# Chunk-wise loading with a k-major first projection, squares on ScalarE, and a later place for the LayerNorm statistics

## The chip, the cores and the metric

The kernel runs on the 8 cores of one Trainium2 chip. Each core takes 2,048 of the 16,384 tokens and does the whole layer for them; the cores exchange nothing. The time is device microseconds of the slowest core. The kernel before takes 786.37 us, the median of 3 runs (785.95 to 786.61).

## The reference

```python
def attn(query):                      # D = 1024, 16 heads of 64, M = 3 levels
    qkv = query @ W_qkv.T + b_qkv
    q, v = qkv[..., :D], qkv[..., 2*D:]            # per head: [B, H, L, 64]
    cq, cv = haar_wavedec(q, 3), haar_wavedec(v, 3)  # along L
    prod = [cq[j]*wq[j] * (cv[j]*wv[j]) for j in range(3)] + [cq[3]*cv[3]]
    a = prod[0]
    for d in prod[1:]:
        a = haar_idwt_step(a, d)
    return a @ W_out.T + b_out
def ffn(x):                           # hidden 3072, int weights * 1/127
    return (silu(x @ wg.T) * (x @ wu.T)) @ wd.T
x = layernorm(x + attn(x))            # LayerNorm 1
x = layernorm(x + ffn(x))             # LayerNorm 2
```

Everything is kept transposed: the 1024 features lie on partitions in 8 chunks of 128, the tokens along the free dimension, in 4 groups (g) of 512. A LayerNorm therefore needs sums over partitions, and these are made on TensorE: a matmul with a matrix that holds 1/1024 everywhere gives the mean (line 548), a second one over the squares the mean square (line 554).

## The kernel before, in words

The kernel is written as a list of operations for each of the five engines. The order of the calls in the Python text is the order of the instructions on each engine, and a small planner (`_Plan.op`) turns the reads and writes of each operation into semaphore waits. An operation may name whole groups of buffers as one resource: `r_ysq` stands for all eight tiles of squares, and `r_ybfp[g % 2]` for the eight bf16 tiles of one token group. DMAs go out on two queues, SyncE's (`DQ`) and GpSimd's (`GQ`); a queue's issues are in the order of the text.

Stage 1, loading and projection. The 8 MB of x come in four DMAs of two chunks each, chunks 0 to 3 on SyncE's queue and 4 to 7 on GpSimd's, and behind them on GpSimd's queue the first weight slabs. Each chunk is cast to bf16, the even ones by ScalarE (line 321), the odd ones by VectorE (line 327). For every output chunk c, `proj_chunk` makes q and then v: for each of the 4 token groups 8 matmuls (k = 0 to 7, line 367) into one of PSUM banks 0 to 3, and one ScalarE eviction (line 374). Then `mixer(c)` runs 18 VectorE operations, the Haar transform, products and the inverse; the first two read all of q and v, and the evictions of the next q wait for them.

Stage 2, output projection and LayerNorm 1. `wout_group(g)` makes 8 output chunks (oc) of 8 matmuls each (line 475). The first group runs k = 0 to 6 of all eight while the last mixer works, and k = 7 afterwards. Behind each chunk stands a tail: ScalarE evicts the bank (line 487), VectorE adds x (line 493), VectorE squares the sum (line 495). Most VectorE operations carry the line of the helper `tt`, line 266. In groups 1 to 3 the tails of the first three chunks are held back, and ahead of them the callback `_mid_stats` puts the statistics of the group before: 16 matmuls into banks 4 and 5, an eviction of the mean (line 563), two VectorE operations for the variance, Ln and Exp on ScalarE (lines 568, 571), one more on VectorE. The statistics of group 3 follow in the FFN, at hc = 1. The normalization of a group, 2 casts and 16 operations on VectorE (lines 588 to 596), is put behind all tails of the next group (`flush_norm`).

Stage 3, the FFN, twice over two token groups: gate and up matmuls (line 722), Silu on ScalarE (line 731), the product on VectorE (line 736); then the down projection, 24 matmuls for each output chunk (line 755). Its tail is an eviction (line 765), steps of LayerNorm 2 of the group before, an add on VectorE (line 771), a cast on ScalarE (line 775) and a square on VectorE (line 779).

Of the kernel before, what the change touches and what calls it, by code (L numbers as in the profile page):

```python
# [10 lines left out]
AF = mybir.ActivationFunctionType  # L11
ALU = mybir.AluOpType
# [107 lines left out]
def _build_nc():  # L120
    nc = bass.Bass("TRN2", target_bir_lowering=False)

    x_d = nc.dram_tensor("x", [128, NCH * TOK], F32, kind="ExternalInput").ap()
    wq_d = nc.dram_tensor("wq", [NCH, 128, 8 * 128], F32, kind="ExternalInput").ap()
# [53 lines left out]
    o_xbf = S0  # L178
# [48 lines left out]
    P = _Plan()  # L227
# [36 lines left out]
    def tt(out, i0, i1, op, reads, writes):  # L264
        P.op("vector", "dve", 1,
             (lambda e, out=out, i0=i0, i1=i1, op=op: e.tensor_tensor(out=out, in0=i0, in1=i1, op=op),  # L266
              tuple(reads), tuple(writes)))
# [38 lines left out]
                                 in_=biasp_d.rearrange("(c p) k -> p c k", p=128)),  # L306
           (), (r_bias,))
    rXdq, rXgq = _Res(), _Res()
    for h in range(4):
        sl = slice(h * 2 * TOK, (h + 1) * 2 * TOK)  # L310
        Q = DQ if h < 2 else GQ
        wr = ((rXc[2 * h], rXc[2 * h + 1])
              + ((rXdq,) if h == 1 else (rXgq,) if h == 3 else ()))
        Q.dma(lambda e, sl=sl: e.dma_start(out=Xflat[:, sl], in_=x_d[:, sl]),
              (), wr)

    xbf = v16(o_xbf, NCH * TOK)
    for c in range(NCH):
        if c % 2 == 0:
            P.op("scalar", "act", 1,  # L320
                 (lambda e, c=c: e.activation(out=xbf[:, c * TOK:(c + 1) * TOK],  # L321
                                              in_=X3[:, c, :], func=AF.Identity,
                                              bias=0.0, scale=1.0),
                  (rXc[c],), (rxbf[c],), tuple(rXg)))
        else:
            P.op("vector", "dve", 1,
                 (lambda e, c=c: e.tensor_copy(xbf[:, c * TOK:(c + 1) * TOK],  # L327
                                               X3[:, c, :]),
                  (rXc[c],), (rxbf[c],), tuple(rXg)))
    P.op("vector", "dve", 1,  # L330
         (lambda e: e.tensor_copy(cons[:, 15:16], cons[:, 5:6]),
          (rXdq, rXgq, r_consts), tuple(rXg)))

    wf3 = v32(o_wfeat, 48).rearrange("p (c k) -> p c k", k=6)
    al3 = v32(o_alpha, 32).rearrange("p (c k) -> p c k", k=4)
# [47 lines left out]
    def mixer(c):  # L383
# [32 lines left out]
        tt(me, a1.rearrange("p (b i) -> p b i", i=4), d1q.rearrange("p (b i) -> p b i", i=4), ALU.add, [rc], [r_mixc[c]])  # L416
        tt(mo, a1.rearrange("p (b i) -> p b i", i=4), d1q.rearrange("p (b i) -> p b i", i=4), ALU.subtract, [rc], [r_mixc[c]])

    for c in range(NCH):
        wap, wres = stream_slab(wq_d[c])  # L420
        proj_chunk(c, wap, wres, qt, r_qt, 0, xbf, rxbf)
        wap, wres = stream_slab(wv_d[c])
        proj_chunk(c, wap, wres, vt, r_vt, 1, xbf, rxbf)
        woap, wores = stream_slab(wo_d[c])
        DQ.dma(lambda e, c=c, woap=woap: e.dma_start(out=wos_d[c], in_=woap),
               (wores,), (r_wos[c],))
        mixer(c)
# [54 lines left out]
    def _wout_tail(g, oc, bank, ybfp):  # L482
        es_ = etmp_rr[0] % 6
        etmp_rr[0] += 1
        tmp = v32(o_etmp + 2048 * es_, TG)
        P.op("scalar", "act", 1,
             (lambda e, bank=bank, tmp=tmp, oc=oc: e.activation(  # L487
                 out=tmp, in_=pb[bank], func=AF.Identity,
                 bias=bias3[:, oc, 2:3], scale=1.0),
              (r_pb[bank], r_bias), (r_etmp[es_],)))  # L490
        xsl = v32(o_X + (oc * TOK + g * TG) * 4, TG)
        ybf_w = [r_ybfp[g % 2]] + (r_wosl_e[2:] if g == 1 else [])
        tt(ybfp[:, oc * TG:(oc + 1) * TG], tmp, xsl, ALU.add,
           [r_etmp[es_], rXg[g]], ybf_w)
        tt(_sq_ap(oc), ybfp[:, oc * TG:(oc + 1) * TG], ybfp[:, oc * TG:(oc + 1) * TG],
           ALU.mult, [r_ybfp[g % 2]], [r_ysq])

    PBANKS = [0, 1, 2, 3, 6, 7, 4, 5]

    def wout_group(g, mid_cb=None):  # L500
        ybfp = v16(o_ybf + 8192 * (g % 2), NCH * TG)
        if g == 0:
            info = {}
            for oc in range(NCH):
                wbf, wres = wout_slab(g, oc)
                bank = PBANKS[oc]
                info[oc] = (bank, wbf, wres)
                _wout_mm(g, oc, bank, wbf, wres, list(range(7)), True, False)
            for oc in range(NCH):
                bank, wbf, wres = info[oc]  # L510
                _wout_mm(g, oc, bank, wbf, wres, [7], False, True)
                _wout_tail(g, oc, bank, ybfp)
            wout_rr[0] = 0
        else:
            held = []
            for oc in range(NCH):
                wbf, wres = wout_slab(g, oc)
                bank = WBANKS[wout_rr[0] % 6]
                wout_rr[0] += 1
                _wout_mm(g, oc, bank, wbf, wres, list(range(8)), True, True)  # L520
                if oc < 3:
                    held.append((oc, bank))
                    if oc == 2:
                        if mid_cb:
                            mid_cb()
                        for hoc, hbank in held:
                            _wout_tail(g, hoc, hbank, ybfp)
                        held = []
                else:
                    _wout_tail(g, oc, bank, ybfp)  # L530
# [166 lines left out]
    for hh in range(2):  # L697
# [41 lines left out]
        for gi in range(2):  # L739
            g = 2 * hh + gi  # L740
            pg = g % 2
            ybase = y2off[pg]
            for oc in range(NCH):
                par = wd_slot[0] % 4
                wd_slot[0] += 1
                GQ.dma(lambda e, oc=oc, par=par: e.dma_start(  # L746
                           out=v16(o_wdbf + 6144 * par, 3072), in_=wd_d[oc]),
                       (), (r_wdbf[par],))
                wdbf_ap = v16(o_wdbf + 6144 * par, 3072)
                bank = dwn_rr[0] % 4  # L750
# [28 lines left out]
                tt(_sq_ap(oc), y2bfp[:, oc * TG:(oc + 1) * TG],
                   y2bfp[:, oc * TG:(oc + 1) * TG], ALU.mult, [r_ybfp[pg]], [r_ysq])  # L780
            pending_stages.extend(ln2_stages(g))

    flush_ln2()
# [73 lines left out]
```

How the kernel before makes its waits and increments, by code:

```python
            def body(h_, eng=eng):  # L789
                for builder, waits, incspec in P.ops[eng]:
                    for s, v in waits:
                        h_.wait_ge(sems[s], v)
                    if builder is not None:
                        ins = builder(h_)
                        if incspec is not None:
                            ins.then_inc(sems[incspec[0]], incspec[1])
```

## Time and profile before

| what | value |
|---|---|
| median of 3 runs | 786.37 us |
| the profiled execution's own time | 787.92 us |
| its span, slowest core (core 6) | 786.3 us (all cores 781.2 to 786.3) |
| PE matmuls busy | 701.7 us, 89% of the span |
| VectorE (DVE) busy | 320.1 us, 41% |
| ScalarE (ACT) busy | 195.0 us, 25% |
| GpSimd (POOL) busy | 65.2 us, 8% |

The page has one column for each fortieth of the span (19.7 us). PE's busy tenths are `0199999978887999999999999999999999999980`, VectorE's `0218888875787521221221225433322211121546`: the first column without matmuls is the load of x, columns 9 to 13 hold stage 2, and the last column is the end of LayerNorm 2. Matmul busy time says that PE had matmuls in flight, not how fast they ran; the granted clock of a stretch stands in rows of its own. L266 is a helper's line, so VectorE rows are told apart by tiles: `t_sc<-t_fsc,t_X` is the add of stage 2, `t_sc<-t_sc 128x512 bf16` there the square.

### The profile page before, as it was taken

Reading aid. Unit: us, or ns where it says so; the run is one execution under the profiler, and the core shown is the slowest. Engines: PE = TensorE matmul, PEld = TensorE weight load, DVE = VectorE, ACT = ScalarE, POOL = GpSimd, SP = SyncE. Lnnn points to the kernel's source line nnn. Section 1 sums busy time; section 2 is a strip of 40 time slices with the busy share of each in tenths; the row PEclk is TensorE's granted clock in tenths of the full one; section 3 lists DMA queues with packets and bytes.
Section 4 is the critical chain, followed back from the end, with each engine's and each line's share of the span. In section 5 each row is a group of like instructions: output and inputs, shape, how many; then the busy total and the mean of one; then the engine's idle time right before and its main releaser. Section 6 shows DMA issues by size and latency. Waiting matters only on the chain.

```text
span 786.3 us, 9771 instructions; the slowest of 8 cores (781.2 to 786.3 us)
## 1 busy us (share of the span) xinstructions
PE 701.7 (89%) x3136; PEld 315.1 (40%) x3200; DVE 320.1 (41%) x524; ACT 195.0 (25%) x295; POOL 65.2 (8%) x113
## 2 busy tenths in 40 slices
PE   0199999978887999999999999999999999999980
PEld 0034444433332444444444444444444444444430
DVE  0218888875787521221221225433322211121546
ACT  0234343324332311111111232331111111123220
POOL 1001011000001011100110101001101111010000
PEclk9999999999997999999999999999999999999995
DMA  8915444353312222222252437223332225244512
GB/s 231 251 28 94 68 81 81 94 150 81 84 49 88 74 81 66 69 81 80 81 188 81 161 121 216 93 80 113 102 108 81 81 80 188 79 140 143 174 55 107
DMA packets 33936, 84.56 MB, mean 108 GB/s; under 512 B 4704, under 2 KB 4704, under 8 KB 33376
## 3 DMA queue, kind: packets, MB, share of 16 engines
q0 software_dynamic: 21408, 60.82, 26.7%
q1 hardware_dynamic: 12480, 23.11, 9.7%
q8 instruction: 28, 0.46, 0.2%
q14 instruction: 20, 0.16, 0.1%
HBM read 54.56 MB, written 10.49 MB: 83 GB/s over the span
## 4 chain that ended last, share of the span: by engine, by line
PE 80%; DVE 10%; DMA 5%; issue 2%; ACT 2%; another core or an unknown queue 0%; DVEq 0%; SPq 0%; ACTq 0%; POOLq 0%
PE pb L722 42%; PE pb L755 20%; PE pb L367 14%; DVE t_sc L266 5%; DMA t_X<-x 4%; PE pb L548 2%; PE pb L554 1%; DVE t_fsc L266 1%; DVE t_ntmp L266 1%; DVE t_ntmpbf L266 1%; PE pb L475 1%; DVE t_var L266 1%; ACT t_sc L321 0%; DMA t_sc<-wgu 0%
## 5 line engine op out<-in xcount | busy, mean ns | idle before, releaser
L722 PE MATMUL pb<-t_sc 128*128 128x512 bf16 x1506 | 332.7, 381 | 6.5 <-DMA t_sc<-wgu 4.9
L722 PEld LDWEIGHTS pb<-t_sc 128*128 128x128 bf16 x1536 | 150.7, 98 | 188.2 <-issue 8.5
L755 PE MATMUL pb<-t_h,t_mix 128*128 128x512 bf16 x752 | 165.2, 379 | 3.6 <-DVE t_h L736 2.8
L736 DVE TENSOR_TENSOR t_h<-pb,t_sg 128x512 bf16<-128x512 f32 x96 | 66.4, 691 | 232.3 <-PE pb L722 221.2
L367 PE MATMUL pb<-t_sc 128*128 128x512 bf16 x502 | 114.7, 388 | 38.6 <-DMA t_sc<-wq 36.4
L731 ACT ACTIVATE t_sg<-pb 128x512 f32<-128x512 f32 x96 | 57.1, 597 | 254.6 <-PE pb L722 237.7
L755 PEld LDWEIGHTS pb<-t_h,t_mix 128*128 128x128 bf16 x768 | 75.0, 98 | 93.7 <-issue 3.6
L266 DVE TENSOR_TENSOR t_sc<-t_sc 128x512 bf16<-128x512 bf16 (+3 forms) x144 | 83.0, 577 | 63.7 <-ACT t_sc L775 30.3
L367 PEld LDWEIGHTS pb<-t_sc 128*128 128x128 bf16 x512 | 50.8, 99 | 102.0 <-issue 44.0
L701 POOL DMA_DIRECT2D t_sc<-wgu x48 | 33.8, 705 | 390.8 <-PE pb L722 287.4
L475 PE MATMUL pb<-t_mix,t_sc 128*128 128x512 bf16 x250 | 58.8, 394 | 8.2 <-ACT t_fsc L487 5.9
L374 ACT ACTIVATE t_sc<-pb,t_bias 128x512 bf16<-128x512 f32 x64 | 44.0, 687 | 69.2 <-PE pb L367 48.9
L475 PEld LDWEIGHTS pb<-t_mix,t_sc 128*128 128x128 bf16 x256 | 25.6, 101 | 41.0 <-issue 13.4
L765 ACT ACTIVATE t_dtmp<-pb 128x512 f32<-128x512 f32 x32 | 19.0, 595 | 91.9 <-PE pb L755 86.0
L266 DVE TENSOR_TENSOR t_X<-t_dtmp,t_sc 128x512 f32<-128x512 f32 x16 | 11.1, 693 | 57.0 <-ACT t_dtmp L765 57.0
L746 POOL DMA_DIRECT2D t_mix<-wd x32 | 17.0, 536 | 158.3 <-PE pb L755 153.6
L548 PE MATMUL pb<-t_sc,t_ones 128*128 128x512 bf16 x63 | 17.1, 416 | 9.0 <-DVE t_sc L266 6.5
L487 ACT ACTIVATE t_fsc<-pb,t_bias 128x512 f32<-128x512 f32 x32 | 19.4, 693 | 18.8 <-PE pb L475 18.1
L266 DVE TENSOR_TENSOR t_sc<-t_fsc,t_X 128x512 bf16<-128x512 f32 x32 | 22.1, 692 | 4.6 <-ACT t_fsc L487 1.6
L327 DVE CAST t_sc<-t_X 128x2048 bf16<-128x2048 f32 x4 | 4.7, 1224 | 30.2 <-DMA t_X<-x 30.2
L554 PE MATMUL pb<-t_sc,t_ones 128*128 128x512 bf16 x63 | 16.4, 406 | 0.0
L266 DVE TENSOR_TENSOR t_fsc<-t_dtmp,t_sc 128x512 f32<-128x512 f32 x16 | 11.0, 690 | 12.9 <-ACT t_dtmp L765 12.4
(39 smaller groups left out, 211.8 us busy)
## 6 DMA issues: line engine op xcount, KB each, us to landing
t_sc<-wgu POOLq DMA_DIRECT2D x48, 512.0 KB, 3.7
t_mix<-wd POOLq DMA_DIRECT2D x32, 768.0 KB, 4.2
t_sc<-wos SPq DMA_DIRECT2D x32, 256.0 KB, 3.0
t_X<-x POOLq DMA_DIRECT2D x2, 2048.0 KB, 21.8
t_X<-x SPq DMA_DIRECT2D x2, 2048.0 KB, 26.3
y<-t_X SPq DMA_DIRECT2D x8, 512.0 KB, 3.7
y<-t_fsc SPq DMA_DIRECT2D x8, 512.0 KB, 2.8
t_sc<-wq POOLq DMA_DIRECT2D x8, 256.0 KB, 5.5
```

The costliest lines, as they stand in the source:

```text
L266: (lambda e, out=out, i0=i0, i1=i1, op=op: e.tensor_tensor(out=out, in0=i0, in1=i1, op=op), tuple(reads), tuple(writes)))
L367: lambda e, bank=bank, k=k, g=g, wbf=wbf: e.matmul(pb[bank], wbf[:, 128 * k:128 * (k + 1)], rhs_ap[:, k * TOK + g * TG: k * TOK + (g + 1) ...
L374: (lambda e, bank=bank, g=g, c=c, dst_ap=dst_ap, bcol=bcol: e.activation(out=dst_ap[:, g * TG:(g + 1) * TG], in_=pb[bank], func=AF.Identit ...
L475: lambda e, bank=bank, k=k, g=g, wbf=wbf, s=start, st=stop, ks=ks: e.matmul(pb[bank], wbf[:, 128 * k:128 * (k + 1)], mix[:, k * TOK + g * ...
L487: (lambda e, bank=bank, tmp=tmp, oc=oc: e.activation(out=tmp, in_=pb[bank], func=AF.Identity, bias=bias3[:, oc, 2:3], scale=1.0), (r_pb[ba ...
L548: parts.append((lambda e, c=c, bm=bm: e.matmul(pb[bm], ones_ap, bfap[:, c * TG:(c + 1) * TG], start=(c == 0), stop=(c == NCH - 1)), (r_one ...
L554: parts.append((lambda e, c=c, bs=bs: e.matmul(pb[bs], ones_ap, _sq_ap(c), start=(c == 0), stop=(c == NCH - 1)), (r_ones, r_ysq), (r_pb[bs ...
L701: GQ.dma(lambda e, hc=hc, par=par: e.dma_start(out=_wgu_slot_ap(par).rearrange("p (w f) -> p w f", f=1024), in_=wgu_d[hc].rearrange("w p f ...
L722: lambda e, bank=bank, wsel=wsel, k=k, g=g, wgubf_ap=wgubf_ap: e.matmul(pb[bank], wgubf_ap[:, wsel * 1024 + 128 * k: wsel * 1024 + 128 * ( ...
L731: (lambda e, gbank=gbank, sgap=sgap: e.activation(out=sgap, in_=pb[gbank], func=AF.Silu, bias=0.0, scale=S_DEQ), (r_pb[gbank],), (r_sg[pid ...
L736: (lambda e, hsl=hsl, sgap=sgap, ubank=ubank: e.tensor_tensor(out=hsl, in0=pb[ubank], in1=sgap, op=ALU.mult), (r_pb[ubank], r_sg[pidx]), ( ...
L755: lambda e, bank=bank, hc=hc, gi=gi, wdbf_ap=wdbf_ap: e.matmul(pb[bank], wdbf_ap[:, 128 * hc:128 * (hc + 1)], h[:, hc * 1024 + gi * TG: hc ...
```

## The change

Four edits. x comes in eight DMAs of one chunk, four on each queue, and the two weight slabs of output chunk 0 are issued ahead of them. Output chunk 0 has a projection of its own, `proj_chunk0`: k is the outer loop and all eight banks (4 for q, 4 for v) accumulate at once; the evictions come with the last k. The squares of stage 2 and of the down projection move from VectorE to ScalarE (activation `Square`), right behind the add or the cast. In groups 1 to 3 of stage 2 six tails are held back, not three, so the statistics stand behind the sixth chunk.

```diff
-    for h in range(4):
-        sl = slice(h * 2 * TOK, (h + 1) * 2 * TOK)
-        Q = DQ if h < 2 else GQ
...
-        Q.dma(lambda e, sl=sl: e.dma_start(out=Xflat[:, sl], in_=x_d[:, sl]),
-              (), wr)
+    def _load_x_and_cast():
+        for c in range(NCH):
+            Q = DQ if c < 4 else GQ
+            wr = (rXc[c],) + ((rXdq,) if c == 3 else (rXgq,) if c == 7 else ())
+            Q.dma(lambda e, c=c: e.dma_start(out=Xflat[:, c * TOK:(c + 1) * TOK],
+                                             in_=x_d[:, c * TOK:(c + 1) * TOK]),
+                  (), wr)
...  (the casts, as before)
+    def proj_chunk0(w0q, w0v):
+        streams = ((w0q[0], w0q[1], qt, r_qt, 0), (w0v[0], w0v[1], vt, r_vt, 1))
+        for k in range(7):
+            for si in range(2):
+                wap, wres = streams[si][0], streams[si][1]
+                for g in range(NG):
+                    bank = 4 * si + g
+                    P.op("tensor", "pe", 1,
+                         (lambda e, bank=bank, k=k, g=g, wap=wap: e.matmul(
+                             pb[bank], wap[:, 128 * k:128 * (k + 1)],
+                             xbf[:, k * TOK + g * TG: k * TOK + (g + 1) * TG],
+                             start=(k == 0), stop=False),
+                          (wres, rxbf[k]), (r_pb[bank],)))
+        for si in range(2):
...
+            for g in range(NG):
+                bank = 4 * si + g
...  (the matmul of k = 7 into this bank, then its eviction by ScalarE)
+        bank_rr[0] = 0
+
+    w0q = stream_slab(wq_d[0])
+    w0v = stream_slab(wv_d[0])
+    _load_x_and_cast()
     for c in range(NCH):
+        if c == 0:
+            proj_chunk0(w0q, w0v)
+        else:
...  (slab q, proj_chunk, slab v, proj_chunk, as before)
         woap, wores = stream_slab(wo_d[c])
...
@@ _wout_tail
-        tt(_sq_ap(oc), ybfp[:, oc * TG:(oc + 1) * TG], ybfp[:, oc * TG:(oc + 1) * TG],
-           ALU.mult, [r_ybfp[g % 2]], [r_ysq])
+        P.op("scalar", "act", 1,
+             (lambda e, oc=oc, ybfp=ybfp: e.activation(
+                 out=_sq_ap(oc), in_=ybfp[:, oc * TG:(oc + 1) * TG],
+                 func=AF.Square, bias=0.0, scale=1.0),
+              (r_ybfp[g % 2],), (r_ysq,)))
@@ wout_group
-                if oc < 3:
+                if oc < 6:
                     held.append((oc, bank))
-                    if oc == 2:
+                    if oc == 5:
@@ the tail of the down projection
-                tt(_sq_ap(oc), y2bfp[:, oc * TG:(oc + 1) * TG],
-                   y2bfp[:, oc * TG:(oc + 1) * TG], ALU.mult, [r_ybfp[pg]], [r_ysq])
+                P.op("scalar", "act", 1,
+                     (lambda e, oc=oc, y2bfp=y2bfp: e.activation(
+                         out=_sq_ap(oc), in_=y2bfp[:, oc * TG:(oc + 1) * TG],
+                         func=AF.Square, bias=0.0, scale=1.0),
+                      (r_ybfp[pg],), (r_ysq,)))
```

## Rows read from the trace of the kernel before

**Rows 1.** The chain that ended last, in order: start us, us, what.
```profile
2.98 32.37 DMA t_X<-x
...
53.39 10.74 PE pb L367 x49
```

**Rows 2.** Timeline of stage 1: start us, us, engine line op xcount, idle before, releaser.
```profile
22.41 1.91 ACT L321 ACTIVATE t_sc<-t_X 128x2048 bf16<-128x2048 f32 x1 [19.46 <-DMA t_X<-x]
35.45 3.50 DVE L327 CAST t_sc<-t_X 128x2048 bf16<-128x2048 f32 x3 [11.80 <-DMA t_X<-x]
56.73 0.69 ACT L374 ACTIVATE t_sc<-pb,t_bias 128x512 bf16<-128x512 f32 x1 [1.04 <-PE pb L367]
57.52 2.56 DVE L266 TENSOR_TENSOR t_sc<-t_sc 128x2048 bf16<-128x2048 bf16 x2 [15.44 <-ACT t_sc L374]
69.37 1.49 DVE L266 TENSOR_TENSOR t_mix<-t_sc 128x1024 bf16<-128x1024 bf16 x2
71.40 1.23 DVE L266 TENSOR_TENSOR t_sc<-t_sc 128x2048 bf16<-128x2048 bf16 x1 [0.53 <-ACT t_sc L374]
```

**Rows 3.** DMA issues of the first 60 us: count, KB each, median us to landing.
```profile
t_X<-x SPq DMA_DIRECT2D x2, 2048.0 KB, 26.3
t_sc<-wv POOLq DMA_DIRECT2D x2, 256.0 KB, 18.8
```

**Rows 4.** Stretches of core 6: PE, PEld, DVE, ACT, POOL busy, PEclk, DMA share, GB/s.
```profile
41.10:46.90 5.80, 5.80 (x14) 2.08 (x15) 0.77 (x4) 1.37 (x2) 0.00 (x0) 1.00 0.00 0
180.00:182.00 2.00, 2.00 (x6) 0.71 (x5) 0.00 (x0) 0.00 (x0) 0.00 (x0) 0.50 0.00 0
```

**Rows 5.** Timeline of stage 2, group 0 and its statistics.
```profile
167.45 6.85 PE L475 MATMUL pb<-t_mix,t_sc 128*128 128x512 bf16 x31 [2.10 <-DVE t_mix L266]
167.92 4.73 ACT L487 ACTIVATE t_fsc<-pb,t_bias 128x512 f32<-128x512 f32 x8 [13.82 <-PE pb L475]
168.78 0.69 DVE L266 TENSOR_TENSOR t_sc<-t_fsc,t_X 128x512 bf16<-128x512 f32 x1 [1.58 <-ACT t_fsc L487]
178.54 0.69 DVE L266 TENSOR_TENSOR t_sc<-t_fsc,t_X 128x512 bf16<-128x512 f32 x1
179.62 3.31 PE L548 MATMUL pb<-t_sc,t_ones 128*128 128x512 bf16 x8 [5.32 <-DVE t_sc L266]
183.03 0.60 ACT L563 ACTIVATE t_msb<-pb 128x512 f32<-128x512 f32 x1 [10.38 <-PE pb L548]
```

**Rows 6.** Timeline of stage 2, groups 1 to 3.
```profile
188.51 4.21 ACT L487 ACTIVATE t_fsc<-pb,t_bias 128x512 f32<-128x512 f32 x7
189.49 0.69 DVE L266 TENSOR_TENSOR t_sc<-t_fsc,t_X 128x512 bf16<-128x512 f32 x1
199.90 0.42 DVE L588 CAST t_rbf<-t_rr 128x512 bf16<-128x512 f32 x1
207.50 0.69 DVE L266 TENSOR_TENSOR t_var<-t_msb 128x512 f32<-128x512 f32 x1
210.43 3.56 ACT L487 ACTIVATE t_fsc<-pb,t_bias 128x512 f32<-128x512 f32 x6
232.52 4.14 ACT L487 ACTIVATE t_fsc<-pb,t_bias 128x512 f32<-128x512 f32 x7
```

**Rows 7.** Timeline of the passage into the FFN, PE.
```profile
243.55 9.34 PE L722 MATMUL pb<-t_sc 128*128 128x512 bf16 x32 [4.92 <-DMA t_sc<-wgu]
256.18 5.99 PE L722 MATMUL pb<-t_sc 128*128 128x512 bf16 x27
```

**Rows 8.** A tail of the down projection, on ACT and DVE.
```profile
755.70 0.69 DVE L266 TENSOR_TENSOR t_fsc<-t_dtmp,t_sc 128x512 f32<-128x512 f32 x1 [3.04 <-ACT t_dtmp L765]
756.54 0.63 ACT L775 ACTIVATE t_sc<-t_fsc 128x512 bf16<-128x512 f32 x1 [1.01 <-DVE t_fsc L266]
762.39 0.43 DVE L266 TENSOR_TENSOR t_sc<-t_sc 128x512 bf16<-128x512 bf16 x1 [0.88 <-ACT t_sc L775]
```

**Rows 9.** Groups of instructions by line: count, busy us, mean ns.
```profile
L568 ACT ACT_TABLE_LOAD x5 | 6.4, 1283 | 10.2 <-DVE t_var L266 10.2
```

More of the change, by code:

```diff
@@ L308, in _build_nc @@
     rXdq, rXgq = _Res(), _Res()
-    for h in range(4):
-        sl = slice(h * 2 * TOK, (h + 1) * 2 * TOK)
-        Q = DQ if h < 2 else GQ
-        wr = ((rXc[2 * h], rXc[2 * h + 1])
-              + ((rXdq,) if h == 1 else (rXgq,) if h == 3 else ()))
-        Q.dma(lambda e, sl=sl: e.dma_start(out=Xflat[:, sl], in_=x_d[:, sl]),
-              (), wr)
-    xbf = v16(o_xbf, NCH * TOK)
[L318 to L329, printed above, removed]
@@ L330, in _build_nc @@
-    P.op("vector", "dve", 1,
-         (lambda e: e.tensor_copy(cons[:, 15:16], cons[:, 5:6]),
-          (rXdq, rXgq, r_consts), tuple(rXg)))
+    xbf = v16(o_xbf, NCH * TOK)
+    def _load_x_and_cast():
[5 more added lines that the diff above has]
+                  (), wr)
+        for c in range(NCH):
+            if c % 2 == 0:
+                P.op("scalar", "act", 1,
+                     (lambda e, c=c: e.activation(out=xbf[:, c * TOK:(c + 1) * TOK],
+                                                  in_=X3[:, c, :], func=AF.Identity,
+                                                  bias=0.0, scale=1.0),
+                      (rXc[c],), (rxbf[c],), tuple(rXg)))
+            else:
+                P.op("vector", "dve", 1,
+                     (lambda e, c=c: e.tensor_copy(xbf[:, c * TOK:(c + 1) * TOK],
+                                                   X3[:, c, :]),
+                      (rXc[c],), (rxbf[c],), tuple(rXg)))
+        P.op("vector", "dve", 1,
+             (lambda e: e.tensor_copy(cons[:, 15:16], cons[:, 5:6]),
+              (rXdq, rXgq, r_consts), tuple(rXg)))
@@ L417, in mixer @@
         tt(mo, a1.rearrange("p (b i) -> p b i", i=4), d1q.rearrange("p (b i) -> p b i", i=4), ALU.subtract, [rc], [r_mixc[c]])
-    for c in range(NCH):
[L420 to L423, printed above, removed]
+    def proj_chunk0(w0q, w0v):
[12 more added lines that the diff above has]
+        for si in range(2):
+            wap, wres, dst, dres, bcol = streams[si]
+            for g in range(NG):
+                bank = 4 * si + g
+                P.op("tensor", "pe", 1,
+                     (lambda e, bank=bank, wap=wap, g=g: e.matmul(
+                         pb[bank], wap[:, 896:1024],
+                         xbf[:, 7 * TOK + g * TG: 7 * TOK + (g + 1) * TG],
+                         start=False, stop=True),
+                      (wres, rxbf[7]), (r_pb[bank],)))
+                P.op("scalar", "act", 1,
+                     (lambda e, bank=bank, g=g, dst=dst, bcol=bcol: e.activation(
+                         out=dst[:, g * TG:(g + 1) * TG], in_=pb[bank],
+                         func=AF.Identity, bias=bias3[:, 0, bcol:bcol + 1],
+                         scale=1.0),
+                      (r_pb[bank], r_bias), (dres,)))
+        bank_rr[0] = 0
+    w0q = stream_slab(wq_d[0])
+    w0v = stream_slab(wv_d[0])
+    _load_x_and_cast()
+    for c in range(NCH):
+        if c == 0:
+            proj_chunk0(w0q, w0v)
+        else:
+            wap, wres = stream_slab(wq_d[c])
+            proj_chunk(c, wap, wres, qt, r_qt, 0, xbf, rxbf)
+            wap, wres = stream_slab(wv_d[c])
+            proj_chunk(c, wap, wres, vt, r_vt, 1, xbf, rxbf)
         woap, wores = stream_slab(wo_d[c])
@@ L494, in _wout_tail @@
            [r_etmp[es_], rXg[g]], ybf_w)
-        tt(_sq_ap(oc), ybfp[:, oc * TG:(oc + 1) * TG], ybfp[:, oc * TG:(oc + 1) * TG],
-           ALU.mult, [r_ybfp[g % 2]], [r_ysq])
+        P.op("scalar", "act", 1,
+             (lambda e, oc=oc, ybfp=ybfp: e.activation(
+                 out=_sq_ap(oc), in_=ybfp[:, oc * TG:(oc + 1) * TG],
+                 func=AF.Square, bias=0.0, scale=1.0),
+              (r_ybfp[g % 2],), (r_ysq,)))
     PBANKS = [0, 1, 2, 3, 6, 7, 4, 5]
@@ L778, in _build_nc @@
                       (r_y2p[pg][oc // 2],), (r_ybfp[pg],)))
-                tt(_sq_ap(oc), y2bfp[:, oc * TG:(oc + 1) * TG],
-                   y2bfp[:, oc * TG:(oc + 1) * TG], ALU.mult, [r_ybfp[pg]], [r_ysq])
+                P.op("scalar", "act", 1,
+                     (lambda e, oc=oc, y2bfp=y2bfp: e.activation(
+                         out=_sq_ap(oc), in_=y2bfp[:, oc * TG:(oc + 1) * TG],
+                         func=AF.Square, bias=0.0, scale=1.0),
+                      (r_ybfp[pg],), (r_ysq,)))
             pending_stages.extend(ln2_stages(g))
```

## The prediction

> **What bounds the kernel now.** I read the page's chain first: 80% of the span is PE, 10% VectorE, 5% DMA. PE is the bound, except in two places where it waits for something else, and the change touches both. The first is the load: the chain begins with 32.37 us of DMA for x, and then PE's matmuls follow each other at 10.74 us for 49, 0.219 us each [rows 1]. The second is stage 2, where the chain runs through VectorE and PE has gaps of 2 to 5 us [rows 5 to 7]. The timeline of both places then gives the durations. The down projection has PE as its bound, with 5.2 us of matmuls (24 at 0.219) over each tail. The reader should see in stage 2 that each group has one cycle: tails, normalization of the group before, variance, Ln and Exp, next tails. From the first eviction of group 1 to that of group 2 it is 188.51 to 210.43, 21.9 us, and to that of group 3 22.1 us [rows 6], while PE needs 80 matmuls, 17.5 us. So whatever lengthens VectorE's and ScalarE's common chain there lengthens the kernel one for one, and whatever PE does there is covered.
>
> **Part 1, the load and chunk 0 (gain).** Before, chunk 0's last eviction starts at 56.73, so its matmuls end at 56.6 [rows 2]. Chunks 0 and 1 of x are in at 22.4 and the rest is cast from 35.45 [rows 2]; on SyncE's queue the two issues take 26.3 us at the median, the later one 32.4 [rows 1, 3]. Afterwards the bytes of both queues are the same; on GpSimd's two slabs only stand ahead of x instead of behind. So chunk 3, last on SyncE's queue, lands at 35.4 as before, and chunk 7 when the second slab landed before. Of the two wv issues in the first 60 us the median landing is 18.8 us [rows 3]; the later one takes 3.8, so the first takes 33.9 from its issue at 3.5, which gives 37.4. VectorE casts 3, 5, 7 from 35.45 (3.50 us for three), the last from 37.4 to 38.6. ScalarE's casts of 2, 4, 6 are done by then, since 2 has its own DMA now, due half way between 22.4 and 35.4.
> Matmuls of k = 0 to 2 (24 of 64) find their chunks at about 17, 24 and 31 us and are hidden in the load. From 36.8 PE has 40 left. Before, the first 14 in a row took 5.80 us, 0.414 each, and only then 0.219 each [rows 1, 4]; the granted clock reads 1.00 there, so the spacing itself must tell, and it is that of half the clock. With PE only in bursts before, I take the same: 5.8 + 26 x 0.219 = 11.5 us, end at 48.3. That is 8.3 us earlier.
> What is late next: all eight evictions now come at the end. The first starts at 46.9, eight at 0.59 each [rows 5] end at 51.7, the mixer starts at 51.9 and its first two operations (2.56 us) end at 54.5. The evictions of chunk 1's q are queued behind them on ScalarE, so its first bank is free at 55.3; PE comes to that bank for v at 48.3 + 32 x 0.219 = 55.3. I charge 0.1. The mixer itself starts 5.6 us earlier, not 8.3, and takes 13.34 us (57.52 to 70.86) against 13.88 from mixer to mixer [rows 2]; with gaps of 0.1 us, it makes up 0.44 a chunk, and seven times 13.44 from 51.9 is 146.0, where PE's pace would have put the last mixer at 146.1. So the debt is just paid. The slab wv of chunk 1 overwrites wq of chunk 0, now read until 47.4, not 50; with 3.8 us to land it is there before 55.3. Part 1: -8.2 us. Bounds: all 40 at 0.219 gives 45.6, -11; if x is late by 2 us and all 40 run at 0.414, the end is at 55.4, -1.2. I take the middle since it is the row nearest to it.
>
> **Part 2, squares on ScalarE in stage 2 (loss).** On VectorE add and square follow each other while ScalarE evicts far ahead: eight evictions in 4.73 us, first to last add 168.78 to 178.54, 1.39 us for each [rows 5], later (189.49 on) 1.33. Afterwards ScalarE's order is evict(0), square(0), evict(1), square(1). square(0) waits for add(0), which waits for evict(0), and evict(1) is queued behind square(0). Nothing overlaps any more. One round: evict start to add start 0.86 (167.92 to 168.78) [rows 5]; add start to the next ScalarE start 0.84, and a ScalarE operation of 128x512 from SBUF 0.63 [rows 8], from which I take 0.1 off for the next eviction, which starts 0.59 after the last where it is free to, though it lasts 0.69. That is 0.86 + 0.84 + 0.54 = 2.24 us for each tail.
> Group 0: add(7) starts at 167.92 + 7 x 2.24 + 0.86 = 184.5 and ends at 185.2; the statistics start at 185.3, not 179.62: +5.7. PE has done six chunks of group 1 by then (bank 7 is evicted at 179.8) and waits 3.7 us. Before, it waited 5.32 and its clock was granted at half (0.50, six matmuls in 2 us) [rows 4], so the eight of line 548 took 3.31 us; I leave that cost in, and take 1.6 us off for the low end. From the statistics to the first eviction of group 1 nothing changes (8.9 us): 194.2.
> Groups 1 and 2: let E be the first eviction. add(0) waits for the product of mean and rstd, E + 0.98 [rows 6]; square(0) at E + 1.82, evict(1) at E + 2.36, evict(7) at E + 15.8, add(7) ends at E + 17.35. From there to the next group's E the rows give 10.5 us (199.90 to 210.43), so the cycle is 27.9 against 21.9: +6.0, twice, and E of group 3 is at 250.0 instead of 232.52, +17.5. The edit of the held tails alone is worth nothing here: the sixth chunk of the next group needs the bank of evict(7) (E + 16.5), so PE starts the statistics at E + 18.3, and the variance is not wanted before E + 25, since VectorE normalizes for 7.6 us [rows 6]. If that cover were gone, it would cost 0.9 us a group.
> Into the FFN: PE's last chunk of group 3 ends near 255.5, the first slab of the FFN comes 4.9 us later and 32 matmuls take 9.34 us at the low clock [rows 7], which gives 269.5. The statistics of group 3 need the last square, at 268.1. The first product of VectorE waits for the normalization of group 2, from 267.4 to 275.0, and frees its bank at 275.8. PE's work of hc = 1, with the gate half done while it waits, is where it would be had it begun at 274.1; before it began at 256.18: +17.9. Bounds: a round of 2.15 to 2.35 us, over 24 rounds that count, -2.2 to +2.6, and the 1.6 above: 14.1 to 20.5.
> That ScalarE keeps its order, the rows show: it sits idle for 10.38 us before 183.03 while three finished banks of group 1, the last of them filled at 174.3, wait for evictions that are queued behind the one of line 563 [rows 5].
> The page "TensorE: Matmul & The Clock Gate" of the Trainium skill (section "Architectural detail: the array is 16× 32×32, not 1× 128×128") says that ScalarE's and VectorE's queues are strictly first in, first out. The trace agrees with its 10.38 us; by a queue that could run ahead the sum would be that of rival (a).
>
> **Part 3, squares in the down projection.** For each tail ScalarE gets 0.63 us more, 1.9 of 5.2 us. At the very end the square on VectorE starts 762.39 [rows 8], right behind the cast; on ScalarE it starts at about the same time and is 0.2 us longer, while PE first makes the 8 matmuls of the mean. Nothing, in both directions up to 0.3 us, as VectorE's steps of normalization would fill the place of the square but the last add is set by the last eviction.
>
> **Sum.** -8.2 + 17.9 = +9.7 us on the profiled execution's 787.92, so 797.6. That execution is 1.55 us above the median 786.37, and I predict for the median 796.1.
>
> **The rivals.**
> (a) The evictions run ahead. ScalarE would evict bank 1 while it waits for add(0), VectorE would be rid of its squares, and a tail would cost 1.13 us (ScalarE's 0.59 + 0.54), not 1.33. Then stage 2 gains 8 x 0.2 = 1.6 us in each of three groups, and the sum is -8.2 - 4.8, 773.4. It decides at one point: whether evict(1) starts before square(0). Against it: the order of the text, and the 10.38 us above. 0.06. A weaker form is that the load gives 11 us or more and a round is under 1.9 us; then the time is 785 or less. 0.05.
> (b) The load gives all and the rounds are short, 786 to 788. 0.04.
> (c) The load gives next to nothing: PE takes k in order, and chunk 3 sits at the end of its queue as before; with chunk 7 late too the sum is -1.2 + 17.9, 803. For it speaks that the DMAs are the bound of that stretch; against it, 24 matmuls surely fit in before 35 us. 0.08.
> (d) Square needs another activation table than Ln and Exp. A load takes 1.283 us [rows 9]. One more in group 0, two each in groups 1 and 2, one in group 3, one at the end: 7 x 1.28 = 9.0, time 805. The trace of before shows that Identity and Ln share a table, since one load serves groups 0 to 2; of Square it shows nothing. 0.07.
> The page "ScalarE: Activation LUTs" (section "Table sets: the hidden batching unit") says that cheap functions come in every set, but names only relu, copy, identity and abs. If Square is one of them, (d) is void; no row here shows it.
>
> **Numbers.** The forecast holds 0.70, with its own range 791 to 802. A difference of 0.2% is about what a measurement of this kernel can tell from none. Faster 0.11 from (a), same 0.04 from (b), slower 0.85. The range is 789 to 803.5: below, it reaches to the bounds -11 and +14.1 (789.5); above, to (c); outside lie (a), (b) and (d).
>
> **What would show it.** The load: the matmuls of chunk 0 in bursts at about 17, 24 and 31 us and without a gap from 36.8 to 48.3; the last mixer at 146. Stage 2: on ScalarE alternate evictions and squares 2.24 us apart, each square with about 0.9 us of idle before it, put down to the add, and 28 us from group to group. Wrong would be evictions in a row without squares between, table loads beside the squares, or a last mixer later than 152.

## The result and the profile after

The changed kernel is slower: 1.0127 times the time of before (95% interval 1.0109 to 1.0146), which is 796.4 us on the 786.4 of before, or +10.0 us. I had forecast +9.7 us, 796.1 (range 789 to 803.5). The three undisturbed runs took 795.5, 797.0 and 797.2 us; three further runs, in which two cores ran at a lower clock, took 815 to 817 and are left out.

The page of the profile after, its head, busy times and the chain's shares:

```profile
span 795.7 us, 9893 instructions; the slowest of 8 cores (791.5 to 795.7 us)
...
PE 714.9 (90%) x3200; PEld 316.2 (40%) x3200; DVE 292.8 (37%) x460; ACT 235.0 (30%) x359; POOL 66.2 (8%) x115
...
PE 76%; DVE 10%; ACT 6%; DMA 4%; issue 3%; SPq 0%; DVEq 0%; ACTq 0%
```

VectorE has lost 27 us of work (320.1 to 292.8), ScalarE has gained 40 us (195.0 to 235.0), and ScalarE now holds 6% of the chain that ends last, where it held 2%. Both engines are busy for less than half of the span, so I looked for the cause in the order of the work and not in its amount.

The timeline of the load and of chunk 0, on core 3, the slowest one. It answers to [rows 2]; L427 is a matmul of k = 0 to 6, L437 one of k = 7, L443 an eviction of chunk 0:

```profile
14.73 1.91 ACT L321 ACTIVATE t_sc<-t_X 128x2048 bf16<-128x2048 f32 x1 [11.78 <-DMA t_X<-x]
16.79 3.57 PE L427 MATMUL pb<-t_sc 128*128 128x512 bf16 x8 [16.79 <-ACT t_sc L321]
22.48 3.57 PE L427 MATMUL pb<-t_sc 128*128 128x512 bf16 x8 [2.12 <-DVE t_sc L327]
29.40 3.57 PE L427 MATMUL pb<-t_sc 128*128 128x512 bf16 x8 [3.35 <-ACT t_sc L321]
33.49 3.50 DVE L327 CAST t_sc<-t_X 128x2048 bf16<-128x2048 f32 x3 [11.27 <-DMA t_X<-x]
34.97 8.89 PE L427 MATMUL pb<-t_sc 128*128 128x512 bf16 x32 [2.00 <-DVE t_sc L327]
...
44.23 5.95 ACT L443 ACTIVATE t_sc<-pb,t_bias 128x512 bf16<-128x512 f32 x8 [11.02 <-PE pb L437]
...
50.28 2.55 DVE L266 TENSOR_TENSOR t_sc<-t_sc 128x2048 bf16<-128x2048 bf16 x2 [12.97 <-ACT t_sc L443]
...
53.87 12.46 PE L367 MATMUL pb<-t_sc 128*128 128x512 bf16 x57 [1.37 <-ACT t_sc L374]
```

On this core three bursts of eight matmuls lie in the load, each at half pace (8 in 3.57 us), and 40 are left when chunk 3 is cast. PE then loses 1.37 us at 53.87, waiting for an eviction that was itself queued behind the mixer's first two operations.

The timeline of stage 2 on the same core. L525 is the eviction, L534 the square; it answers to [rows 5] and [rows 6]:

```profile
167.72 0.67 ACT L525 ACTIVATE t_fsc<-pb,t_bias 128x512 f32<-128x512 f32 x1
168.56 0.69 DVE L266 TENSOR_TENSOR t_sc<-t_fsc,t_X 128x512 bf16<-128x512 f32 x1 [1.53 <-ACT t_fsc L525]
169.41 0.63 ACT L534 ACTIVATE t_sc<-t_sc 128x512 bf16<-128x512 bf16 x1 [1.01 <-DVE t_sc L266]
169.94 0.67 ACT L525 ACTIVATE t_fsc<-pb,t_bias 128x512 f32<-128x512 f32 x1
...
176.62 3.57 PE L589 MATMUL pb<-t_sc,t_ones 128*128 128x512 bf16 x8 [3.98 <-DVE t_sc L266]
179.99 2.92 PE L595 MATMUL pb<-t_sc,t_ones 128*128 128x512 bf16 x8
...
186.49 0.67 ACT L525 ACTIVATE t_fsc<-pb,t_bias 128x512 f32<-128x512 f32 x1
...
214.12 0.67 ACT L525 ACTIVATE t_fsc<-pb,t_bias 128x512 f32<-128x512 f32 x1
```

Read the first four rows as one round: eviction at 167.72, add at 168.56, square at 169.41, next eviction at 169.94. The round is 2.22 us, and each engine sits idle while the other works: VectorE 1.53 us ahead of each add, ScalarE 1.01 us ahead of each square. The first eviction of group 2 starts 27.6 us after that of group 1, 21.9 before.

Where the time went, stage by stage. The milestones were read from the timelines of all eight cores; the table has the means, in us.

| from | to | before | after | difference | forecast |
|---|---|---|---|---|---|
| start | last mixer begins | 151.86 | 142.51 | -9.35 | -8.2 |
| last mixer | Exp of group 0 | 33.74 | 40.53 | +6.8 | +5.7 |
| Exp, group 0 | Exp, group 1 | 21.92 | 27.62 | +5.7 | +6.0 |
| Exp, group 1 | Exp, group 2 | 22.08 | 27.44 | +5.4 | +5.8 |
| Exp, group 2 | statistics of the last group | 530.06 | 532.73 | +2.7 | +0.4 |
| those statistics | end of the span | 23.98 | 22.59 | -1.4 | 0 |
| sum | | 783.64 | 793.42 | +9.8 | +9.7 |

### The profile page after: what moved, and what is told of

It reads as the page before. It is cut to its first block, busy times and chain, and to the rows that moved or that the text cites. A ratio compares the mean times of both kernels' runs of the same rounds, so it can differ in the third digit from the quotient of the medians.

```text
span 795.7 us, 9893 instructions; the slowest of 8 cores (791.5 to 795.7 us)
## 1 busy us (share of the span) xinstructions
PE 714.9 (90%) x3200; PEld 316.2 (40%) x3200; DVE 292.8 (37%) x460; ACT 235.0 (30%) x359; POOL 66.2 (8%) x115
## 4 chain that ended last, share of the span: by engine, by line
PE 76%; DVE 10%; ACT 6%; DMA 4%; issue 3%; SPq 0%; DVEq 0%; ACTq 0%
PE pb L763 40%; PE pb L796 21%; PE pb L367 11%; DVE t_sc L266 5%; DMA t_X<-x 4%; ACT t_fsc L525 2%; PE pb L589 1%; ACT t_sc L534 1%; PE pb L595 1%; PE pb L427 1%; DVE t_ntmpbf L266 1%; DVE t_fsc L266 1%; DVE t_var L266 1%; DVE t_ntmp L266 1%; ACT t_sc L443 1%
## 5 line engine op out<-in xcount | busy, mean ns | idle before, releaser
L763 PEld LDWEIGHTS pb<-t_sc 128*128 128x128 bf16 x1536 | 150.6, 98 | 190.1 <-issue 11.0
L796 PE MATMUL pb<-t_h,t_mix 128*128 128x512 bf16 x768 | 166.4, 379 | 2.6 <-DVE t_h L777 2.6
L513 PE MATMUL pb<-t_mix,t_sc 128*128 128x512 bf16 x256 | 65.9, 419 | 21.5 <-ACT t_fsc L525 19.3
L367 PEld LDWEIGHTS pb<-t_sc 128*128 128x128 bf16 x448 | 43.8, 98 | 54.5 <-issue 1.8
L266 DVE TENSOR_TENSOR t_sc<-t_sc 128x512 bf16<-128x512 bf16 (+3 forms) x80 | 55.8, 697 | 24.6 <-ACT t_sc L443 13.0
L374 ACT ACTIVATE t_sc<-pb,t_bias 128x512 bf16<-128x512 f32 x56 | 38.4, 688 | 56.1 <-PE pb L367 33.3
L427 PE MATMUL pb<-t_sc 128*128 128x512 bf16 x56 | 19.6, 523 | 24.3 <-ACT t_sc L321 20.1
L266 DVE TENSOR_TENSOR t_sc<-t_fsc,t_X 128x512 bf16<-128x512 f32 x32 | 22.1, 692 | 45.1 <-ACT t_fsc L525 45.0
L534 ACT ACTIVATE t_sc<-t_sc 128x512 bf16<-128x512 bf16 x32 | 20.2, 630 | 33.4 <-DVE t_sc L266 33.4
L525 ACT ACTIVATE t_fsc<-pb,t_bias 128x512 f32<-128x512 f32 x32 | 21.5, 672 | 13.9 <-PE pb L513 13.9
L589 PE MATMUL pb<-t_sc,t_ones 128*128 128x512 bf16 x64 | 16.8, 410 | 6.4 <-DVE t_sc L266 4.0
```

The costliest lines, as they stand in the source:

```text
L367: lambda e, bank=bank, k=k, g=g, wbf=wbf: e.matmul(pb[bank], wbf[:, 128 * k:128 * (k + 1)], rhs_ap[:, k * TOK + g * TG: k * TOK + (g + 1) ...
L374: (lambda e, bank=bank, g=g, c=c, dst_ap=dst_ap, bcol=bcol: e.activation(out=dst_ap[:, g * TG:(g + 1) * TG], in_=pb[bank], func=AF.Identit ...
L427: (lambda e, bank=bank, k=k, g=g, wap=wap: e.matmul(pb[bank], wap[:, 128 * k:128 * (k + 1)], xbf[:, k * TOK + g * TG: k * TOK + (g + 1) * TG],
L513: lambda e, bank=bank, k=k, g=g, wbf=wbf, s=start, st=stop, ks=ks: e.matmul(pb[bank], wbf[:, 128 * k:128 * (k + 1)], mix[:, k * TOK + g * ...
L525: (lambda e, bank=bank, tmp=tmp, oc=oc: e.activation(out=tmp, in_=pb[bank], func=AF.Identity, bias=bias3[:, oc, 2:3], scale=1.0), (r_pb[ba ...
L534: (lambda e, oc=oc, ybfp=ybfp: e.activation(out=_sq_ap(oc), in_=ybfp[:, oc * TG:(oc + 1) * TG], func=AF.Square, bias=0.0, scale=1.0), (r_y ...
```

## The experiments

Ratios are against the kernel before, run in turn on the same chip. Five rounds each.

**Each edit alone.** Four kernels, each with one edit of the change on the kernel before.

> The loading and chunk 0 edits alone, squares on VectorE, three tails held, as before. Serial-tail theory (all the loss is in the squares of stage 2): the last mixer starts 9.4 us earlier in the mean of the cores, as in the changed kernel (151.9 to 142.5), nothing else moves: about 777.2 us, ratio 0.988. Rival, that the gain of the load is given back later (the mixers or the slabs of stage 2 are late): ratio 0.995 to 1.0.

> Only the squares of stage 2 on ScalarE, each right behind its add; load, held tails (three) and down projection as before. Serial-tail theory: rounds of 2.22 us, group cycles of 27.5 us, first statistics 6 to 7 us later, passage into the FFN 1 to 3 us longer: +18 to +20.5 us, ratio 1.023 to 1.026. Rival, that a good part of the loss comes from the later place of the statistics (six tails held): +12 us or less.

> Only the held tails: six, not three. With squares on VectorE PE would fill its 5.3 us gap ahead of the first statistics with three more chunks, so its clock stays up there and the 16 matmuls take 3.5 us, not 5.1: -1.6 us, ratio 0.998. Rival, that the sixth chunk makes the statistics of groups 1 and 2 late: by the rows of before PE would end them about 1 us before the variance is wanted; if it does not, up to +2 us.

> Only the squares of the down projection on ScalarE. Forecast: hidden under 5.2 us of matmuls for each tail: ratio 1.000 within 0.001. Rival, that VectorE without its squares ends LayerNorm 2 sooner, or that the last statistics (3.6 us in the changed kernel, 5.1 before) owe their speed to it: -1.3 us, ratio 0.998.

| kernel | ratio | 95% interval | us |
|---|---|---|---|
| load and chunk 0 only | 0.9875 | 0.9860 to 0.9890 | -9.8 |
| squares of stage 2 only | 1.0237 | 1.0223 to 1.0251 | +18.6 |
| six held tails only | 1.0004 | 0.9995 to 1.0013 | +0.3 |
| squares of the down projection only | 1.0008 | 0.9999 to 1.0017 | +0.6 |

They add up to +9.7; the whole change measured +10.0. The load's gain arrives in full, and all of the loss is in the squares of stage 2. The second kernel's trace has the stages of the changed one, in the mean of its cores: 40.0 us from the last mixer to the first Exp, then cycles of 27.6 and 27.4 us. The down projection's squares move nothing that can be told from zero.

The six held tails missed their expectation of -1.6 us, and the trace says how. PE on core 0 of that kernel:

```profile
177.53 1.89 PE L548 MATMUL pb<-t_sc,t_ones 128*128 128x512 bf16 x8
179.26 1.89 PE L554 MATMUL pb<-t_sc,t_ones 128*128 128x512 bf16 x8
185.55 16.53 PE L475 MATMUL pb<-t_mix,t_sc 128*128 128x512 bf16 x64 [4.40 <-ACT t_fsc L487]
201.93 1.89 PE L548 MATMUL pb<-t_sc,t_ones 128*128 128x512 bf16 x8
```

The first statistics do run at full pace (1.89 us for eight, 3.31 before, [rows 5]): in the mean of the cores that stage is 1.1 us shorter. But then PE has nothing left to do while ScalarE makes Ln and Exp, idles 4.4 us, and starts the next 64 matmuls at half pace (granted clock 0.50 from 185.5 to 189 us): 16.5 us for all of them. So the statistics of group 1 are late (VectorE, done with its normalization, waits 0.80 and 0.41 us for their two parts), and the two cycles are 22.8 and 22.4 us, not 21.9 and 22.1. What was won in front was given back behind.

**The order on ScalarE.** Is it the place of the square, or the square itself? The squares stay on ScalarE, but one step later.

```diff
 # stage 2 of the changed kernel, order on ScalarE
-evict(0) square(0) evict(1) square(1) evict(2) ...
+evict(0) evict(1) square(0) evict(2) square(1) ...
 # the sixth experiment also: resource of each bf16 sum
-            [r_etmp[es_], rXg[g]], [r_ybfp[g % 2]]
+            [r_etmp[es_], rXg[g]], [r_ybo[g % 2][oc]]   # r_ybfp too for oc 0 and 7
```

> The changed kernel with one thing moved: in stage 2 ScalarE evicts chunk oc + 1 before it squares chunk oc. The bf16 sums of a group are still one resource, so add(oc + 1) waits for square(oc). Serial-tail theory (the loss is the order on ScalarE): a round is square 0.63, then add 0.69 and two hand-overs of 0.15, 1.65 us instead of 2.22, 4.5 us less in each of three groups and about 1 us less at the passage: 796.1 - 14 = 782 us, ratio 0.995. Rival, that ScalarE's Square itself (0.63 against 0.42 us) or its share of the memory ports makes the loss: 792 us or more.

> As the run before, but each bf16 sum has a resource of its own, so add(oc + 1) waits only for its eviction. Serial-tail theory: the round is set by ScalarE alone, 0.59 + 0.54 = 1.13 us, below the 1.33 of the kernel before: 1.6 us less in each of three groups than before the change, with the load's 9.8: 786.4 - 9.8 - 4.8 = 772 us, ratio 0.982. Rival as above: 785 us or more.

The fifth kernel has a ratio of 0.9937 (0.9923 to 0.9950), 781.2 us: 15 us came back for one exchanged pair of lines. Its rows show the wait that is left, the add behind the square of the chunk before (L539 is the square), and rounds of 1.64 us:

```profile
186.31 0.69 DVE L266 TENSOR_TENSOR t_sc<-t_fsc,t_X 128x512 bf16<-128x512 f32 x1 [0.95 <-ACT t_sc L539]
187.15 0.63 ACT L539 ACTIVATE t_sc<-t_sc 128x512 bf16<-128x512 bf16 x1 [0.43 <-DVE t_sc L266]
187.68 0.67 ACT L525 ACTIVATE t_fsc<-pb,t_bias 128x512 f32<-128x512 f32 x1
187.95 0.69 DVE L266 TENSOR_TENSOR t_sc<-t_fsc,t_X 128x512 bf16<-128x512 f32 x1 [0.95 <-ACT t_sc L539]
```

The sixth has 0.9856 (0.9834 to 0.9877), 775.0 us (its runs scatter more than others'). The rounds are 1.10 us, close to the 1.13 expected, but the time is 3 us above what I expected, no better than the load edits alone. In its second cycle on core 5 PE's statistics are the last to come (L608):

```profile
193.00 0.43 DVE L266 TENSOR_TENSOR t_sc<-t_ntmpbf,t_mrbf 128x512 bf16<-128x512 bf16 x1
193.71 1.89 PE L608 MATMUL pb<-t_sc,t_ones 128*128 128x512 bf16 x8
...
196.40 0.69 DVE L266 TENSOR_TENSOR t_var<-t_msb 128x512 f32<-128x512 f32 x1 [2.97 <-ACT t_msb L623]
```

VectorE has done everything by 193.4 and waits 2.97 us for the mean, which stands behind six chunks on PE. The first statistics are late for the same reason: on this core the last square of group 0 ends at 166.4 and PE begins them at 169.16, behind the sixth chunk. That made the held tails the next thing to test.

**The held tails again**, with serial squares (the changed kernel) and with squares one step later.

```diff
-                if oc < 6:
+                if oc < 3:
                     held.append((oc, bank))
-                    if oc == 5:
+                    if oc == 2:
```

> The changed kernel with three tails held, not six. Forecast of the prediction: with serial squares the place of the statistics is worth nothing, the ratio stays at 1.0127 within 0.001. Rival, that six held tails cost here what they cost in the third experiment's groups 1 and 2 (0.9 and 0.4 us): ratio 1.011.

> The sixth experiment with three held tails. Its trace has VectorE waiting 3.0 us for the statistics of group 1, which stand behind the sixth chunk of group 2 on PE. Theory: that wait is the missing gain; with three held PE has the statistics before VectorE wants them, cycles fall to 20.3 us: 772.5 us, ratio 0.982. Rival, that PE's clock, which falls in the longer gaps of group 0, takes it back: 776 us, ratio 0.987.

With serial squares: 1.0153 (1.0138 to 1.0167), more than the 0.001 that I had allowed, though the interval overlaps that of the changed kernel. Its mean cycles are 27.63 and 27.45 us against 27.62 and 27.44, so in the stage concerned the edit is worth nothing, as the prediction said; of the 2 us of difference 0.4 lie in the first statistics, the rest behind stage 2, where the edit changes nothing; it is not explained. With squares one step later: 0.9784 (0.9770 to 0.9797), 769.7 us, 3 us better than I expected, with cycles of 19.85 us against 22.4 and 20.9 with six held. I had looked at the cycles alone; the stage up to the first Exp is 2.4 us shorter too (31.0 against 33.4). The same edit is worth nothing or 6 us, according to what else sets the stage.

**The parts of the load.** Both kernels have the loading edits of the first experiment; one has the old order of matmuls, the other the old place of the slabs.

```diff
 # seventh
-            proj_chunk0(w0q, w0v)
+            proj_chunk(0, w0q[0], w0q[1], qt, r_qt, 0, xbf, rxbf)
+            proj_chunk(0, w0v[0], w0v[1], vt, r_vt, 1, xbf, rxbf)
 # eighth
-    w0q = stream_slab(wq_d[0])
-    w0v = stream_slab(wv_d[0])
     _load_x_and_cast()
+    w0q = stream_slab(wq_d[0])
+    w0v = stream_slab(wv_d[0])
```

> Load edits of the first experiment, but chunk 0 in the old order (all k of one bank, then the next); squares and held tails as before. Theory: the gain comes from k-major, since bank by bank PE cannot pass k = 3 before 34 us and then does 7 of 8 banks, 60 of 64 matmuls; what is left is that the slab is there when x is (PE starts 1 to 2 us earlier): ratio 0.997 to 1.000, against 0.9875 with k-major. Rival, that the early slabs and the single-chunk DMAs make the gain: ratio 0.990 or less.

> Load edits of the first experiment with k-major, but the two slabs of chunk 0 issued behind x, as before. Theory: PE cannot start before the first slab, at 34 to 36 us, and q and v are interleaved, so not before the second, 1 us later; then 64 matmuls in a row, 14 of them at half pace, 16.7 us, as before, and the evictions late on top: ratio 1.000 to 1.003. So neither edit has the gain alone. Rival, that the single-chunk DMAs alone bring 3 us or more: ratio 0.996 or less.

0.9961 (0.9948 to 0.9973) and 0.9968 (0.9957 to 0.9979), so -3.1 and -2.5 us. I had expected less of the first and nothing of the second. What they share is the single-chunk DMA, and the rows of the eighth, core 7, show what it does by itself:

```profile
28.46 5.51 ACT L321 ACTIVATE t_sc<-t_X 128x2048 bf16<-128x2048 f32 x3 [10.70 <-DMA t_X<-x]
34.78 3.50 DVE L327 CAST t_sc<-t_X 128x2048 bf16<-128x2048 f32 x3 [11.33 <-DMA t_X<-x]
35.21 14.34 PE L427 MATMUL pb<-t_sc 128*128 128x512 bf16 x56 [35.21 <-DMA t_sc<-wq]
```

Chunk 2 is cast when it lands and 4 and 6 behind it, so ScalarE's 5.51 us of casts are over when the last chunk comes. Before, they began with it (35.4) and PE had its steady stream only at 41.1 [rows 4]. The first mixer of the eighth starts no earlier than before (55.1 us in the mean of the cores in both), since the evictions come at the end; the last one starts 2.2 us earlier. The other 7 us of the 9.8 need both edits at once: the slabs in front and k outermost. Without the other, neither lets PE do more than a few matmuls inside the load (seven on core 0 of the seventh kernel, none in the eighth).

The place of the slabs has a second effect. VectorE's cast of chunk 3, which starts when the chunk lands, starts at 33.9 us in the mean of the cores of the eighth kernel and at 31.2 in the first experiment, where the slabs stand ahead of x on GpSimd's queue. Chunk 3 is on the other queue and comes earlier; chunk 7, behind the slabs, is cast from 35.4 on, but PE wants it last.

**What the experiments point to.** PE takes k in the order of the text, so chunk 3, last on its queue, holds up 4 and 5, which have landed. Chunk 6 lands about with it: in the first experiment its cast starts at 31.7 us in the mean, that of chunk 3 at 31.2. The expectation below counts it among those that have landed.

```diff
-        for k in range(7):
+        for k in (0, 4, 1, 5, 2, 6, 3):
 # casts in the order 0, 4, 1, 5, 2, 6, 3, 7; 0, 1, 2 on ScalarE, the others on VectorE
```

> The load of the first experiment with k in the order in which the chunks land (0, 4, 1, 5, 2, 6, 3, 7; casts in the same order, 0, 1, 2 on ScalarE), squares and held tails as before. Theory: PE takes k in the order of its text, so 40 of 64 matmuls wait for chunk 3 although 4, 5, 6 have landed; in landing order 16 are left: 24 x 0.22 = 5.3 us and up to 2 us of half pace less: 770 us, ratio 0.980. Rival, that the late mixer (it starts when all evictions are done and has 0.44 us a chunk to make up) caps the gain: ratio 0.985 or more.

> Both together: k in the order of landing, squares on ScalarE behind the next eviction with a resource for each sum, three tails held. If the two gains lie in different stages and add up: 786.3 - 9.8 - 5 - 4 = 767 us, ratio 0.975. Rival: each hides part of the other, 771 us or more, ratio 0.981.

The load edits with this order: 0.9812 (0.9799 to 0.9826), 771.8 us, 5 us better than with k in rising order. I had expected 770, with 16 matmuls left behind chunk 3; since chunk 6 comes no earlier there are 24, and 8 at 0.22 are 1.8 us, about what is missing. The last mixer starts at 137.8 in the mean of the cores, 14 us earlier than before. With the tenth experiment's stage 2 as well: 0.9742 (0.9728 to 0.9756), 766.5 us, where I had expected 767. That is 20 us faster than the kernel before and 30 faster than the changed one, and it keeps all four ideas of the change except the six held tails. PE on core 1 of it, the load and the first statistics (L437 is k = 7):

```profile
14.27 3.57 PE L427 MATMUL pb<-t_sc 128*128 128x512 bf16 x8 [14.27 <-ACT t_sc L321]
21.45 9.74 PE L427 MATMUL pb<-t_sc 128*128 128x512 bf16 x32 [3.61 <-DVE t_sc L327]
32.63 3.61 PE L427 MATMUL pb<-t_sc 128*128 128x512 bf16 x16 [1.44 <-DVE t_sc L327]
36.08 1.89 PE L437 MATMUL pb<-t_sc 128*128 128x512 bf16 x8
...
46.25 89.95 PE L367 MATMUL pb<-t_sc 128*128 128x512 bf16 x416 [1.37 <-ACT t_sc L374]
```

Of chunk 0 eight matmuls are left when the last chunk is cast, at 36.1. In the mean of the cores the first mixer begins at 43.3 us, 47.3 in the first experiment; PE's wait of 1.37 us behind the evictions is still there, and would be the next thing to take away. Measured apart, the load gives 9.8 + 5.0 us and stage 2 with its three held tails 7.2 (0.9784 against 0.9875); that is 22.0, and together they give 20.3. The difference of 1.7 us is about what the intervals leave open; in the traces the stage up to the first Exp is 1.4 us longer in this kernel than in the tenth (32.4 against 31.0).

## Why the prediction was right

- **The load, -8.2 forecast, -9.35 measured** (-9.8 alone). On core 3 the bursts came at 16.8, 22.5 and 29.4 us, as forecast, and the 40 matmuls left took 10.5 us, not 11.5: the stretch at half pace was shorter. One premise failed: I let chunk 3 land as before, but in the mean of the cores its cast starts at 31.2 us, 33.5 before. So the 40 matmuls start at 32.7 in the mean; I had 36.8 on a core whose chunk 3 was 1.9 us later than the mean, so they are 2.2 us early. Two errors go the other way. I took 0.59 us for each of the eight evictions from a row whose outputs are float32 [rows 5]; these took 5.95 us for eight, 0.74 each. So the mixer's first operations end later, and the wait of PE that I put at 0.1 us is 1.37. With these terms (2.2 and 1.0 us more gain, 1.3 less) the sum would be -10.1; the 0.8 us to -9.35 I can't assign, so the term is near in part by luck. That the mixers make up their late start was right: first to last mixer takes 94.5 us, 96.8 before, and the stage ends on PE's pace.
- **The serial round, 2.24 forecast, 2.22 measured.** This is the step on which everything hung, and it came from rows of before alone; its parts are 0.84, 0.85 and 0.53 us where I had 0.86, 0.84 and 0.54. The fifth kernel shows that it is the order and not the operation: the same squares at the same 0.63 us cost 15 us less.
- **ScalarE does not run ahead**, rival (a). In the rows above no eviction starts before the square ahead of it, though the banks are full. The page "TensorE: Matmul & The Clock Gate" of the Trainium skill (section "Architectural detail: the array is 16× 32×32, not 1× 128×128") has ScalarE's and VectorE's queues strictly first in, first out; the trace after agrees, with 1.01 us of idle time ahead of each square.
- **The first statistics, +5.7 forecast, +6.8 measured.** The gap of PE ahead of them was 3.98 us, near my 3.7. The first eight matmuls took 3.57 us at a granted clock of 0.50, the next eight 2.92 at 0.63 in the mean (before 3.31 and 2.19). I had left the cost of before in and not thought that it could grow.
- **The cycles, 27.9 us forecast for each, measured 27.6 and 27.4**, so +5.7 and +5.4. I wrote "+6.0, twice", but the second cycle took 22.1 us before, not 21.9, so there it is +5.8, as in my sum of +17.5. Seven rounds of 2.22 us where I had 2.24 make 0.14 us of the difference.
- **The passage into the FFN, +0.4 forecast, +2.7 measured.** This step failed in size. I let PE do its gate matmuls while the first product waits and charged nothing after that. PE on core 3:

```profile
252.87 9.16 PE L763 MATMUL pb<-t_sc 128*128 128x512 bf16 x32 [4.65 <-DMA t_sc<-wgu]
...
267.39 5.34 PE L763 MATMUL pb<-t_sc 128*128 128x512 bf16 x24 [0.18 <-PE pb L763]
...
274.20 7.98 PE L763 MATMUL pb<-t_sc 128*128 128x512 bf16 x35 [1.47 <-ACT t_sg L772]
```

  The Silu of the next chunk is behind two table loads, and the Ln and Exp between them wait for the variance of group 3, which VectorE makes after it has normalized group 2. So there is a second wait, of 1.47 us, one step behind the one that I followed. It is most of the 2.3 us that I missed; the wait that I did follow is 0.18 us on this core and 0.83 on core 0.
- **The end, 0 forecast, -1.4 measured.** In five of the eight cores the last 16 matmuls ran at full pace (1.89 us for eight), in none before (2.5 to 3.0). PE's wait ahead of them is 2.41 us in both. Why is open. The fourth experiment, with the same squares on ScalarE, does not have it (24.2 us for the end), and the second, whose down projection is that of before, has the full pace in five cores too, so it is not the edit of the down projection.
- **Held tails, 0 forecast:** shown in the cycles of the changed kernel, and shown not to hold in general. Where their cover is gone I had put 0.9 us a group; it was 0.9 and 0.4 us in the third experiment, and 2.5 and 1.0 between the sixth and the tenth.
- **Tables, rival (d):** void. The loads are as many as before (five at Ln [rows 9], four at Silu) and none has the line of a square. Here are the loads of Ln and of Silu:

```profile
L609 ACT ACT_TABLE_LOAD x5 | 6.4, 1283 | 13.8 <-DVE t_var L266 13.8
L772 ACT ACT_TABLE_LOAD x4 | 5.1, 1283 | 0.1
```

  The page "ScalarE: Activation LUTs" of the Trainium skill (section "Table sets: the hidden batching unit") says that cheap functions come in every set, without naming Square among them. These rows bear it out for Square beside Identity, Ln and Exp.
- **Rival (c)**, that the load gives next to nothing, fell with the first experiment.

So the sum was good to 0.3 us, but in part by luck: the load gave 1.2 us more than forecast, the end 1.4, and the cycles cost 0.7 less, while the first statistics and the passage cost 3.4 more.

## What to carry to other kernels

An operation moved to an idle engine takes a place in that engine's order. Write the order down for two rounds and ask what stands behind each wait: in the second experiment 14 us of VectorE's work (320.1 to 306.3) went to an engine busy for 25% of the span, and the kernel lost 18.6 us, because each square waited for an operation on the other engine with the next eviction behind it. One step of software pipelining (the square behind the next eviction) and a resource for each buffer, not for each group, turned the same move into a gain. When a cycle is shared by three engines, an edit that is worth nothing while one of them is the bound can cost 6 us when it no longer is, so try such edits again after each gain.

## What the runs showed that I had not expected

Filling a gap of PE with matmuls from behind it moves the gap. Six held tails took the 5.3 us gap away ahead of the first statistics, and a gap of 4.4 us opened behind them, after which 64 matmuls took 16.5 us instead of 14.0. And the pace in the load differs from core to core. In the changed kernel on core 3 bursts of eight matmuls with gaps of 2 to 3.4 us all stayed at half pace (3.57 us for eight, three times); on cores 1, 2, 4 and 5 the second burst ran at full pace (1.89 us). The gap ahead of it does not decide that: on core 4 it was 1.66 us, and on core 0, where the burst took 3.57 us, 1.31. What does is open. In the landing order, on core 1 of the last kernel, 32 matmuls that began 3.6 us after the last ones took 9.74 us, 0.30 us each, so part of them ran at full pace before the load was over.
